# A fourth step of expert tables, after sample 13, and an output join in two parts

## The chip, the cores and the metric
One core of one Trainium2 chip. Engines: PE (TensorE), DVE (VectorE), ACT (ScalarE), POOL (GpSimd), and SP (SyncE), which issues the plain DMAs; POOL issues the indirect ones. The metric is device time in microseconds (us), lower is better.

## The reference
Sixteen samples of 128 tokens, width 256, pass through two decoder layers. Layer 0: a decayed linear recurrence, cross attention with 16 heads, a feed-forward in FP4. Layer 1: linear attention with a GELU feed-forward, cross attention, and a mixture of experts; a layer norm follows each. Only the last one matters here:

```
logits = xf @ gate_w + gate_b;  probs = softmax(logits)
gates, expert_idx = top_k(probs, 2)              # 2 of 8 experts for each of 2048 tokens
out = sum over the two experts of gate * (relu(x @ w1[e] + b1[e]) @ w2[e] + b2[e])
x = layernorm(x + out)
```

## The kernel before, in words
**Samples.** Six slots hold samples at a time; slot s runs samples s, s+6, s+12. Samples 13 to 16 are therefore the last to run. (Samples are numbered from 1 in the text and from 0 in the code, as n.)

**Routing.** When a sample is done, the router (`pe_router`, `dve_router`) finds its two experts for each token and the row that each pair takes in the expert's region of `xs_d` in HBM. POOL sends the sample's 128 rows there twice, by indirect DMA (L1744 in `pool_router`, then L1756 in `pool_second`, which waits for the first to land). The rank matmuls (L988, L989) give the positions and the running count of pairs per expert, `base`.

**Tiles.** The pairs are worked off in tiles of 128 rows of one expert. As the split over experts is known only at run time, a table (`dve_table`) lists row and expert for each tile. There is a table after each of STEPS = [8, 12, 16] samples, with 9, 8 and 22 tiles (39). The tables after 8 and 12 samples list full tiles alone, as many as there must be in any case; the last table lists all that is left. For a tile SP loads the rows (`rows`, L1885) and the expert's weights in two halves of 512 KB (`load up` L1890, `load down` L1894); PE transposes the rows (`turn`), multiplies by w1 (`up`) and by w2 (`down`); ACT applies bias, relu and the gate (L1615, L1608); POOL sends the 128 results back to the tokens' rows of `ys_d` by indirect DMA (`store`, L1778). Tiles of the first two tables share two buffers of weights, those of the last table have six (HOME, ROOM), four of which (in `PT` and `KB`) come free with the samples and are loaded at once ("early").

**Join.** `join_turns` orders the end. `fetch`: SP waits for the stores of all tiles and loads three rows for each token of a sample, the two expert results and the token with its expert biases, 384 KB (L1864). `add`: POOL adds the first result (L1766). `join`: DVE adds the second and takes mean and variance (L1362 to L1367), POOL the inverse root (L1626), and ACT subtracts the mean (L1589). `finish`: ACT scales (L1593) and SP writes the sample out (L1867). The 16 fetches stand first; then add n+1, join n, finish n-1 follow each other.

**Order.** Each engine runs its instructions in one fixed order. `orders_of` makes it: every piece of work has a listed cost and needs (`plan_*`), and at each step the piece that can start first in this plan is taken, the tiles' pieces last where two tie. The plan knows neither the data nor real times; on the chip an instruction waits for its semaphores, and all that stands behind it on that engine waits with it.

Of the kernel before, what the change touches and what calls it, by code (L numbers as in the profile page):

```python
# [7 lines left out]
ALU = mybir.AluOpType  # L8
# [38 lines left out]

STEPS = [8, 12, B]
SURE = [0, *(2 * m - E + 1 for m in STEPS[:-1]), 2 * B + E - 1]
# [3 lines left out]
REGION = B * P  # L53
NTMAX = max(TILES)
ZROWS = 2048

# [10 lines left out]
CONST = [("cos", DH), ("sin", DH), ("ident", P), ("block", P), ("mask8", HC), ("dest", 2 * B), ("dump", 8), ("iota", E), ("kkeep", 1),  # L67
         ("kminus", 1), ("before", P), ("region", E), ("tiles", NTMAX)]

# [421 lines left out]
def decoder_kernel(nc, xg, xTg, cTg, wts, w4gu, w4dn, rows, cols, const, moe_w, moe_b2, zeros, out):  # L491
# [14 lines left out]
    with ExitStack() as ctx:  # L506
# [47 lines left out]
        for buffers, width in ((XS, XW), (XST, D), (YB, D), (HM, EHC * P)):  # L554
            for i in range(2):
# [18 lines left out]
        base = sb("base", E)  # L574
        cnt = sb("cnt", 6, E + 1)
        below = sb("below", NTMAX, E)
        tcol = sb("tcol", 3, NTMAX)
# [25 lines left out]

        lg_ready, pr_ready, picked, idx_ready, tab_ready, directed, redirected, placed, halved, joined, var6, centred, root6, out_ready = (
            sem(n) for n in ("lg_ready", "pr_ready", "picked", "idx_ready", "tab_ready", "directed", "redirected", "placed",
                             "halved", "joined", "var6", "centred", "root6", "out_ready"))
        gated = sem("gated")
# [79 lines left out]
        def join_rows(n):  # L687
            if n < B // 2:
                return KB_all[:, 3 * D * n:3 * D * (n + 1)]
            j = n - B // 2  # L690
            return slot_rows[:, :, :, :].rearrange("p s a b -> p (s a b)")[:, 3 * D * j:3 * D * (j + 1)]

# [565 lines left out]
        def dve_router(k):  # L1258
            e = k.e
            for n in range(B):  # L1260
# [26 lines left out]
                k.wait_ge(filled[u.at], u.full)  # L1287
                run = base[:, :] if n else k_("region")
                placed = k.step(e.tensor_tensor(lg[:, :], ps[:, u.at, 0:E], run, ALU.add))
# [7 lines left out]
                for t in step_at(n):  # L1297
                    dve_table(k, t)
                    yield

        def dve_table(k, t):


            e, nt, full = k.e, TILES[t], t < len(STEPS) - 1
            c, end, begin, step, had, row0 = (cnt[:, i, 0:E] for i in range(6))
            region, top = k_("region"), float(E * REGION // P)
            hit, tiles = below[0:1, 0:nt, :], k_("tiles")[0:1, 0:nt]
# [4 lines left out]
            k.after(k.step(e.tensor_tensor(c, base[:, :], region, ALU.subtract)))  # L1312
            k.after(k.step(e.tensor_scalar(c, c, 1.0 / P, -half if full else half, ALU.mult, ALU.add)))
            k.after(k.step(e.tensor_scalar(c, c, ROUND, None, ALU.add)))
            k.after(k.step(e.tensor_scalar(c, c, ROUND, None, ALU.subtract)))
            if t:
                k.after(k.step(e.tensor_tensor(c, c, had, ALU.subtract)))
            k.after(k.step(e.tensor_tensor_scan(end, ones[:, 0:E], c, 0.0, ALU.mult, ALU.add)))
            k.step(e.tensor_tensor(hit, bc(end[0:1, :].unsqueeze(1), nt, E), bc(tiles.unsqueeze(2), nt, E), ALU.is_le))
            k.step(e.tensor_scalar(cnt[:, 5, E:E + 1], end[:, E - 1:E], -1.0, top, ALU.mult, ALU.add))  # L1320
            k.after(k.step(e.tensor_tensor(begin, end, c, ALU.subtract)))
            k.after(k.step(e.scalar_tensor_tensor(out=row0, in0=region, scalar=1.0 / P, in1=begin, op0=ALU.mult,
                                                  op1=ALU.subtract)))
            if t:
                k.after(k.step(e.tensor_tensor(row0, row0, had, ALU.add)))
            k.after(k.step(e.tensor_tensor(step, cnt[:, 5, 1:E + 1], row0, ALU.subtract)))
            k.after(k.step(e.tensor_reduce(owner, hit, AX.X, ALU.add)))
            k.after(k.step(e.tensor_tensor(hit, hit, bc(step[0:1, :].unsqueeze(1), nt, E), ALU.mult)))
            k.after(k.step(e.tensor_reduce(gone, hit, AX.X, ALU.add)))
            k.after(k.step(e.scalar_tensor_tensor(out=rows_, in0=gone, scalar=row0[0:1, 0:1], in1=tiles, op0=ALU.add,  # L1330
                                                  op1=ALU.add)))
            k.after(k.step(e.tensor_scalar(tab[t][0:1, 0, :], rows_, float(P), None, ALU.mult)))
            e.tensor_scalar(tab[t][0:1, 1, :], owner, float(E - 1), float(P), ALU.min, ALU.mult).then_inc(tab_ready, 1)
            if full:
                k.after(k.step(e.tensor_scalar(end, end, float(nt), None, ALU.min)))
                k.after(k.step(e.scalar_tensor_tensor(out=begin, in0=begin, scalar=float(nt), in1=end, op0=ALU.min,
                                                      op1=ALU.subtract)))
                if t:
                    k.after(k.step(e.tensor_tensor(had, had, begin, ALU.subtract)))
                else:  # L1340
                    k.after(k.step(e.tensor_scalar(had, begin, -1.0, None, ALU.mult)))

        def dve_bias(k):
# [9 lines left out]
        def dve_join(k):  # L1353
            e = k.e
            for what, n in join_turns():
                if what == "join":
                    v, rows_ = mv2[:, n % 8, :], join_rows(n)
                    x6 = rows_[:, 2 * D:3 * D]
                    k.wait_ge(halved, n + 1)
# [223 lines left out]

        def act_join(k):
            for what, n in join_turns():
                v, x6 = mv2[:, n % 8, :], join_rows(n)[:, 2 * D:3 * D]
                if what == "join":
                    k.wait_ge(var6, 2 * n + 2)
                    k.e.activation(x6, x6, ACT.Identity, scale=1.0, bias=v[:, 6:7]).then_inc(centred, 1)  # L1589
                elif what == "finish":  # L1590
                    k.wait_ge(centred, n + 1)
                    k.wait_ge(root6, n + 1)
                    k.e.activation(x6, x6, ACT.Identity, scale=v[:, 7:8], bias=0.0).then_inc(out_ready, 1)  # L1593
                yield

        def act_tiles(k):
# [163 lines left out]
        def pool_join(k):  # L1760
            for what, n in join_turns():
# [5 lines left out]
                elif what == "join":  # L1767
                    k.wait_ge(var6, 2 * n + 2)
                    pool_root(k, mv2[:, n % 8, :]).then_inc(root6, 1)
# [165 lines left out]
        def idle():  # L1935
            yield from ()
# [15 lines left out]
        @block.scalar  # L1952
        def _(e):
            k = Program(e, None)
            act_start(k)
            in_order("A", [*slots_of(k, act_sample), act_weights(k), act_fold(k), act_router(k), idle(), act_bias(k), act_join(k), idle(), act_tiles(k)])

# [87 lines left out]
```

## Time and profile before

| | us |
|---|---|
| median of 3 runs (995.23 to 997.38) | 996.99 |
| the profiled execution, its own time | 998.28 |
| its span, first to last instruction | 995.2 |
| PE busy in the span | 868.6 (87%) |
| DVE busy | 615.4 (62%) |
| ACT busy | 497.9 (50%) |
| POOL busy | 297.1 (30%) |

Times in the rows are microseconds from the start of the span. The engines' shares are means over stages which differ much: samples with the tiles of the first two tables up to 853.5, then the tiles of the last table, then the join. What a part costs is read in its own stage.

### The profile page before, as it was taken

The page shows a single profiled execution, that of the slowest core. Times are in us where ns is not written, and L with a number is a line of the kernel's source. Part 1 is how long each engine was busy: PE and PEld are TensorE (multiplying, and loading weights), DVE is VectorE, ACT ScalarE, POOL GpSimd, SP SyncE. Part 2 cuts the span into 40 slices and gives each one's busy share as a digit, 9 for nine tenths or more (in the row PEclk, how much of TensorE's full clock was granted, in tenths as well). Part 3 has the DMA queues.
Part 4 walks back from the last instruction along what each step waited for, and adds up shares of the span by engine and source line. Part 5 has one row for each costly group of instructions (what it writes and reads, how often), then busy time and mean ns, then how long its engine had stood idle before and what let it go on. Part 6 is the DMA issues. An engine that isn't in the chain of part 4 may idle for free.

```text
span 995.2 us, 19709 instructions
## 1 busy us (share of the span) xinstructions
PE 868.6 (87%) x7316; PEld 688.7 (69%) x7316; DVE 615.4 (62%) x1840; ACT 497.9 (50%) x1159; POOL 297.1 (30%) x478
## 2 busy tenths in 40 slices
PE   3669899999999899999999999999999999299950
PEld 2446668667777666777678777877877888289940
DVE  4998776676765768866848685778854434200016
ACT  2335446553656454553465545565555555045535
POOL 4423322222343123431213333232421214212236
PEclk9679999999999989999999999999999999689985
DMA  8996000000010000000000030231121226699836
GB/s 323 400 323 210 2 1 12 12 7 17 17 33 28 18 7 17 22 22 17 6 2 22 23 118 23 91 118 54 55 84 54 92 91 212 225 318 351 321 129 235
DMA packets 35950, 102.33 MB, mean 103 GB/s; under 512 B 4984, under 2 KB 20352, under 8 KB 35296
## 3 DMA queue, kind: packets, MB, share of 16 engines
q1 hardware_dynamic: 32448, 91.74, 27.0%
q0 software_dynamic: 3408, 9.34, 2.5%
q8 instruction: 58, 0.95, 0.4%
q14 instruction: 36, 0.29, 0.1%
HBM read 87.53 MB, written 33.35 MB: 121 GB/s over the span
## 4 chain that ended last, share of the span: by engine, by line
PE 63%; DVE 19%; ACT 7%; issue 6%; DMA 3%; POOL 1%; SPq 0%; ACTq 0%; DVEq 0%; POOLq 0%
PE ps L705 44%; PE ps L710 7%; PE ps L717 5%; PE ps L781 3%; DVE PT L1104 2%; DVE stat L1045 2%; ACT PT L1438 2%; ACT slot_rows L1438 1%; PE ps L848 1%; DMA xs_d<-X,idx 1%; PE ps L1006 1%; DVE sm L1061 1%; DVE PT L1069 1%; DMA KB<-xs_d 1%; DVE stat L1046 1%
## 5 line engine op out<-in xcount | busy, mean ns | idle before, releaser
L1626 POOL TENSOR_TENSOR stat<-stat,mhalf 128x1 f32<-128x1 f32 x112 | 67.1, 599 | 291.2 <-DVE stat L1047 291.1
L705 PE MATMUL ps<-wall,slot_rows 128*128 128x256 f32 (+1 forms) x448 | 132.3, 424 | 11.3 <-ACT KB L1465 8.9
L705 PEld LDWEIGHTS ps<-wall,slot_rows 128*128 128x128 f32 x448 | 79.1, 193 | 36.0 <-issue 22.8
L710 PE MATMUL ps<-cst,PT 128*128 128x128 f32 x512 | 73.4, 280 | 14.9 <-DVE PT L1104 4.2
L717 PE MATMUL ps<-KB 32*128 32x128 f32 (+1 forms) x2048 | 76.9, 287 | 7.2 <-DVE PT L1104 2.4
L1104 DVE TENSOR_REDUCE PT<-ps 128x8 f32<-128x1024 f32 x64 | 75.3, 1219 | 12.5 <-PE ps L717 12.4
L705 PE MATMUL ps<-wgu,slot_rows 128*128 128x352 f32 x256 | 82.1, 473 | 0.8 <-ACT slot_rows L1400 0.6
L717 PEld LDWEIGHTS ps<-KB 32*128 32x128 f32 (+1 forms) x2048 | 64.9, 190 | 25.7 <-issue 20.6
L705 PEld LDWEIGHTS ps<-slot_rows,wall 128*128 128x128 f32 x640 | 75.8, 193 | 8.5 <-issue 4.1
L705 PE MATMUL ps<-slot_rows,wall 128*128 128x128 f32 x640 | 79.6, 279 | 1.8 <-DVE KB L1165 0.9
L710 PEld LDWEIGHTS ps<-cst,PT 128*128 128x128 f32 x512 | 58.7, 143 | 30.6 <-issue 16.2
L705 PEld LDWEIGHTS ps<-wgu,slot_rows 128*128 128x128 f32 x256 | 48.9, 195 | 27.6 <-issue 4.8
L705 PE MATMUL ps<-wall,cT 128*128 128x512 f32 x128 | 64.0, 624 | 0.1
L1400 ACT COPY slot_rows<-ps 128x256 f32<-128x256 f32 x96 | 35.5, 378 | 49.3 <-PE ps L710 48.8
L705 PE MATMUL ps<-wall,PT 128*128 128x256 f32 x256 | 58.3, 381 | 1.2 <-ACT PT L1520 1.2
L1692 POOL TENSOR_TENSOR KB<-PT,sm 128x352 f32<-128x352 f32 x32 | 26.4, 826 | 95.3 <-DVE PT L1069 95.2
L705 PEld LDWEIGHTS ps<-wall,PT 128*128 128x128 f32 x256 | 47.4, 190 | 7.8 <-ACT PT L1520 1.4
L1045 DVE BATCH_NORM_STATS2 stat<-slot_rows 128x6 f32<-128x256 f32 x112 | 47.9, 427 | 3.8
L705 PE MATMUL ps<-wdn,PT 128*128 128x256 f32 x192 | 48.1, 392 | 0.3 <-ACT PT L1493 0.3
L705 PE MATMUL ps<-work,EW 128*128 128x128 f32 x368 | 45.2, 276 | 2.0 <-ACT PT L1438 1.7
L705 PEld LDWEIGHTS ps<-work,EW 128*128 128x128 f32 x368 | 43.0, 192 | 2.6 <-ACT PT L1438 1.9
L705 PE MATMUL ps<-EW,work 128*128 128x256 f32 x184 | 44.0, 382 | 0.6 <-DMA EW<-moe_w 0.6
(237 smaller groups left out, 1817.5 us busy)
## 6 DMA issues: line engine op xcount, KB each, us to landing
EW<-moe_w SPq DMA_DIRECT2D x23, 514.0 KB, 4.3
EW<-moe_w SPq DMA_DIRECT2D x23, 512.0 KB, 5.0
PT<-moe_w SPq DMA_DIRECT2D x12, 514.0 KB, 5.9
PT<-moe_w SPq DMA_DIRECT2D x12, 512.0 KB, 6.9
wall<-wts SPq DMA_DIRECT2D x1, 4104.0 KB, 20.4
work<-xs_d SPq DMA_DIRECT2D x25, 129.0 KB, 3.3
KB<-ys_d SPq DMA_DIRECT2D x8, 384.0 KB, 5.9
slot_rows<-ys_d SPq DMA_DIRECT2D x8, 384.0 KB, 9.3
```

Of the source, the lines that this page charges most:

```text
L705: last = k.e.matmul(o, a, b, start=(i == 0), stop=(i == len(pairs) - 1))
L710: last = k.e.transpose(ps[:, u.at, c * P:(c + 1) * P], src[:, c * P:(c + 1) * P], ident)
L717: last = k.e.matmul(ps[:, at, c * P:(c + 1) * P], lhsT[lane, c * P:(c + 1) * P], rhs[lane, c * P:(c + 1) * P], start=True, stop=True)
L781: last = k.e.matmul(ps[lane:lane + HR, u.at, c:c + P], VS[:, s, h * (DH + 1):h * (DH + 1) + HR], exps(s, a, i // HC)[:, i % HC * P:(i % HC ...
L848: last = k.e.transpose(ps[0:kw[i], u.at + i // 4, (i % 4) * P:(i % 4 + 1) * P], KB[s][:, i * P:i * P + kw[i]], ident)
L1006: k.e.matmul(ps[:, u.at, 0:D], gT[0:E, :], b2m[0:E, :], start=True, stop=True).then_inc(filled[u.at], 1)
L1045: k.after(k.step(e.bn_stats(v[:, 0:6], src)))
L1104: e.tensor_reduce(peak[:, 2 * p:2 * p + 2, :, DH], s4, AX.X, ALU.max).then_inc(emptied[u.at], 1)
L1400: k.e.copy(dst, v3(ps[:, u.at, 0:D], P)).then_inc(emptied[u.at], 1)
L1438: e.activation(v3(exps(s, a, p), 512), ps[:, u.at:u.at + 2, :], ACT.Exp, scale=DH ** -0.5).then_inc(emptied[u.at], 1)
L1626: return k.e.tensor_tensor(v[:, 7:8], v[:, 8:9], mhalf[:, :], ALU.pow)
L1692: e.tensor_tensor(h, y, bc(sm[:, s, j, 1, 0:m].unsqueeze(2), m, DH), ALU.mult).then_inc(gpsimd[s], 1)
```

## The change
- STEPS gets 13: the tables come after 8, 12, 13 and 16 samples and list 9, 8, 2 and 20 tiles, 39 as before.
- The last table lists tiles in two groups, first those that hold a pair of samples 1 to 13 (at most SHOWN = 33 tiles in all are then done), then the others. It works on 16 columns instead of 8, and its scratch lies in `w("oT")`.
- Fetches of samples 1 to 13 wait for the first 33 tiles only. The join runs as two parts, samples 1 to 13 and 14 to 16, so its pieces can stand between those of the last 6 tiles.
- The fetches of 14 to 16 stand in SP's order behind the output of sample 11 (n = 10).
- ACT has no part in the join any more: the last step is one DVE instruction, (x - mean) * root, and the instruction that negated the mean is gone. `centred` is gone too.
- Rows of the join lie elsewhere: ten samples in `slot_rows`, the rest from the end of `KB`.

```diff
-STEPS = [8, 12, B]
+STEPS = [8, 12, 13, B]
...
+SEEN = STEPS[-2]
+SHOWN = 2 * SEEN + E - 1
...
 def join_turns():
-    yield from (("fetch", n) for n in range(B))
-    yield "add", 0
-    for n in range(B):
-        if n < B - 1:
-            yield "add", n + 1
-        yield "join", n
-        if n:
-            yield "finish", n - 1
-    yield "finish", B - 1
+    for lo, hi in ((0, SEEN), (SEEN, B)):
+        if not lo:
+            yield from (("fetch", n) for n in range(lo, hi))
+        yield "add", lo
+        for n in range(lo, hi):
+            if n < hi - 1:
+                yield "add", n + 1
+            yield "join", n
+            if n == SEEN - 1:
+                yield from (("fetch", m) for m in range(SEEN, B))
+            if n > lo:
+                yield "finish", n - 1
+        yield "finish", hi - 1
+
+def tiles_of(n):
+    return SHOWN if n < SEEN else NT
...
 def plan_join():
-                        needs=[(n, "saved"), ("table", len(STEPS) - 1), *(("stored", x) for x in range(NT))])
+                        needs=[(n, "saved"), ("table", len(STEPS) - 1), *(("stored", x) for x in range(tiles_of(n)))])
-            yield piece(work=[("D", 1.4, None), ("a", 0.4, None), ("P", 0.57, (n, "last root"))], needs=[(n, "halved")],
-                        alone=True)
+            yield piece(work=[("D", 1.2, None), ("P", 0.57, (n, "last root"))], needs=[(n, "halved")], alone=True)
-            yield piece(work=[("A", 0.4, None), ("S", 0.5, None), ("Q", 0.4, None), ("L", 2.0, (n, "out"))],
+            yield piece(work=[("D", 0.42, None), ("S", 0.5, None), ("Q", 0.4, None), ("L", 2.0, (n, "out"))],
...
+        def dve_counts(k, out, half):
+            e = k.e
+            k.after(k.step(e.tensor_tensor(out, base[:, :], k_("region")[:, 0:E], ALU.subtract)))
+            k.after(k.step(e.tensor_scalar(out, out, 1.0 / P, half, ALU.mult, ALU.add)))
+            k.after(k.step(e.tensor_scalar(out, out, ROUND, None, ALU.add)))
+            k.after(k.step(e.tensor_scalar(out, out, ROUND, None, ALU.subtract)))
...
         def dve_table(k, t):
+            parts = 1 if full else 2
+            wide = parts * E
...
+                k.step(e.tensor_tensor(c[:, E:wide], c[:, E:wide], seen, ALU.subtract))
+                k.after(k.step(e.tensor_tensor(c[:, 0:E], seen, had, ALU.subtract)))
...
+            if not full:
+                k.after(k.step(e.tensor_scalar(gone, owner, float(E), -float(E), ALU.is_ge, ALU.mult)))
+                k.after(k.step(e.tensor_tensor(owner, owner, gone, ALU.add)))
...
+            if STEPS[t] == SEEN:
+                dve_counts(k, seen, half)
...
         def dve_join(k):
-                    e.tensor_scalar(v[:, 6:7], v[:, 6:7], -1.0, None, ALU.mult).then_inc(var6, 1)
+                elif what == "finish":
+                    k.wait_ge(root6, n + 1)
+                    e.tensor_scalar(x6, x6, v[:, 6:7], v[:, 7:8], ALU.subtract, ALU.mult).then_inc(out_ready, 1)
...
-        def act_join(k):
...
         def sp_join(k):
-                    for x in range(NT):
+                    for x in range(tiles_of(n)):
                         k.wait_ge(ys_stored[HOME["store"][x][0]], 16 * HOME["store"][x][2])
```

## Rows read from the trace of the kernel before

**Rows 1.** Busy time by stage: window and length, then PE PEld DVE ACT POOL, clock, DMA, GB/s.
```profile
787.00:800.00 13.00, 13.00 (x143) 11.80 (x143) 1.33 (x7) 8.90 (x21) 3.21 (x6) 1.00 0.51 161
843.00:853.50 10.50, 9.48 (x58) 8.01 (x56) 3.13 (x19) 4.32 (x14) 3.93 (x4) 1.00 0.59 194
853.50:873.00 19.50, 0.59 (x2) 0.18 (x2) 4.12 (x21) 0.06 (x1) 3.42 (x6) 0.54 0.72 263
873.00:876.00 3.00, 2.92 (x12) 2.50 (x13) 0.73 (x5) 0.93 (x4) 0.00 (x0) 0.50 1.01 311
888.00:950.00 62.00, 62.00 (x431) 57.69 (x430) 2.23 (x14) 33.20 (x119) 15.54 (x17) 1.00 0.87 312
```

**Rows 2.** The chain that ended last: start, us, what.
```profile
858.38 6.14 DMA xs_d<-X,idx
...
865.32 7.60 DMA KB<-xs_d
...
934.49 0.22 PE ps L710 x2
934.71 3.52 PE ps L705 x24
...
962.16 3.11 DMA KB<-ys_d
```

**Rows 3.** Time line 842 to 859: start, us, engine, line, what, idle before.
```profile
842.95 2.85 SPq L1894 DMA_DIRECT2D EW<-moe_w  x2
844.53 0.96 POOL L1778 DMA_INDIRECT ys_d<-work,place  x1 [0.31 <-issue]
850.55 1.97 PE L705 MATMUL ps<-EW,work 128*128 128x256 f32 x8 [0.58 <-DMA EW<-moe_w]
852.35 0.28 PE L988 MATMUL ps<-mask,cst 128*128 128x8 f32 x2
853.59 0.16 DVE L1312 TENSOR_TENSOR cnt<-base,cst 128x8 f32<-128x8 f32 x1
853.78 0.96 POOL L1778 DMA_INDIRECT ys_d<-work,place  x1 [1.59 <-ACT work L1608]
855.95 0.32 DVE L1327 TENSOR_REDUCE tcol<-below 1x22 f32<-1x176 f32 x1
857.50 0.17 DVE L1333 TENSOR_SCALAR tab<-tcol 1x22 uint32<-1x22 f32 x1
858.39 0.34 SPq L1890 DMA_DIRECT2D PT<-moe_w  x1
```

**Rows 4.** POOL's time line, two stores of tiles of the second table.
```profile
815.07 1.04 POOL L1778 DMA_INDIRECT ys_d<-work,place  x1 [1.91 <-ACT work L1608]
823.39 0.96 POOL L1778 DMA_INDIRECT ys_d<-work,place  x1 [7.28 <-ACT work L1608]
```

**Rows 5.** Time line of the last tiles (the first two lines: tiles 33 and 39).
```profile
938.26 0.47 ACT L1608 ACTIVATE KB<-ps,gate 128x256 f32<-128x256 f32 x1 [0.59 <-PE ps L705]
938.40 0.33 SPq L1894 DMA_DIRECT2D KB<-moe_w  x1
939.50 0.96 POOL L1778 DMA_INDIRECT ys_d<-KB,place  x1 [2.78 <-DVE place L1378]
...
959.67 0.96 POOL L1778 DMA_INDIRECT ys_d<-KB,place  x1 [0.77 <-ACT KB L1608]
962.16 3.65 SPq L1864 DMA_DIRECT2D KB<-ys_d  x8
```

**Rows 6.** DMA issues from 937 to 941 and after 960: count, KB each, median us to landing.
```profile
ys_d<-KB,place POOLq DMA_INDIRECT x1, 5.1
...
slot_rows<-ys_d SPq DMA_DIRECT2D x8, 384.0 KB, 9.3
```

**Rows 7.** The join's groups (by form): count, busy us, mean ns, idle before.
```profile
L1626 POOL TENSOR_TENSOR mv<-mv,mhalf 128x1 f32<-128x1 f32 x16 | 9.6, 603 | 2.9 <-DVE mv L1367 2.9
...
L1766 POOL TENSOR_TENSOR slot_rows<-slot_rows 128x256 f32<-128x256 f32 x8 | 5.8, 720 | 0.0
```

**Rows 8.** Time line of the join, its first and its last.
```profile
966.09 0.42 DVE L1362 TENSOR_TENSOR KB<-KB 128x256 f32<-128x256 f32 x1 [27.23 <-POOL KB L1766]
...
967.23 0.15 DVE L1366 TENSOR_SCALAR mv<-mv 128x1 f32<-128x1 f32 x1
967.30 0.14 DVE L1367 TENSOR_SCALAR mv<-mv 128x1 f32<-128x1 f32 x1
...
988.22 0.15 DVE L1366 TENSOR_SCALAR mv<-mv 128x1 f32<-128x1 f32 x1
```

**Rows 9.** One line's instructions: duration min/median/max in ns, first and last start.
```profile
L1056 DVE TENSOR_SCALAR X<-slot_rows,stat x16: 399/408/734, 244.7 to 842.3; 128x256 f32<-128x256 f32 x16
```

More of the change, by code:

```diff
@@ L67 @@
 CONST = [("cos", DH), ("sin", DH), ("ident", P), ("block", P), ("mask8", HC), ("dest", 2 * B), ("dump", 8), ("iota", E), ("kkeep", 1),
-         ("kminus", 1), ("before", P), ("region", E), ("tiles", NTMAX)]
+         ("kminus", 1), ("before", P), ("region", 2 * E), ("tiles", NTMAX)]
 def spans(table):
@@ L574, in decoder_kernel @@
         base = sb("base", E)
-        cnt = sb("cnt", 6, E + 1)
-        below = sb("below", NTMAX, E)
+        cnt = sb("cnt", 6, 2 * E + 1)
+        below = sb("below", max(TILES[:-1]), E)
         tcol = sb("tcol", 3, NTMAX)
@@ L1287, in dve_router @@
                 k.wait_ge(filled[u.at], u.full)
-                run = base[:, :] if n else k_("region")
+                run = base[:, :] if n else k_("region")[:, 0:E]
                 placed = k.step(e.tensor_tensor(lg[:, :], ps[:, u.at, 0:E], run, ALU.add))
@@ L1299, in dve_router @@
                     yield
+        def dve_counts(k, out, half):
[4 more added lines that the diff above has]
+            k.after(k.step(e.tensor_scalar(out, out, ROUND, None, ALU.subtract)))
         def dve_table(k, t):
             e, nt, full = k.e, TILES[t], t < len(STEPS) - 1
-            c, end, begin, step, had, row0 = (cnt[:, i, 0:E] for i in range(6))
-            region, top = k_("region"), float(E * REGION // P)
-            hit, tiles = below[0:1, 0:nt, :], k_("tiles")[0:1, 0:nt]
+            parts = 1 if full else 2
+            wide = parts * E
+            c, end, begin, step, gone0, row0 = (cnt[:, i, 0:wide] for i in range(6))
+            had, seen = cnt[:, 4, 0:E], cnt[:, 4, E:2 * E]
+            region, top = k_("region")[:, 0:wide], float(E * REGION // P)
+            late = v3(w("oT")[:, 0:nt * wide], wide)
+            hit, tiles = (below[0:1, 0:nt, :] if full else late[0:1, :, :]), k_("tiles")[0:1, 0:nt]
             owner, gone, rows_ = (tcol[0:1, i, 0:nt] for i in range(3))
@@ L1311, in dve_table @@
             k.wait_ge(emptied[u.at], u.out)
[L1312 to L1320, printed above, removed]
+            dve_counts(k, c[:, wide - E:wide], -half if full else half)
+            if full:
+                if t:
+                    k.after(k.step(e.tensor_tensor(c, c, had, ALU.subtract)))
+            else:
+                k.step(e.tensor_tensor(c[:, E:wide], c[:, E:wide], seen, ALU.subtract))
+                k.after(k.step(e.tensor_tensor(c[:, 0:E], seen, had, ALU.subtract)))
+            k.after(k.step(e.tensor_tensor_scan(end, ones[:, 0:wide], c, 0.0, ALU.mult, ALU.add)))
+            k.step(e.tensor_tensor(hit, bc(end[0:1, :].unsqueeze(1), nt, wide), bc(tiles.unsqueeze(2), nt, wide), ALU.is_le))
+            k.step(e.tensor_scalar(cnt[:, 5, wide:wide + 1], end[:, wide - 1:wide], -1.0, top, ALU.mult, ALU.add))
             k.after(k.step(e.tensor_tensor(begin, end, c, ALU.subtract)))
@@ L1324, in dve_table @@
             if t:
-                k.after(k.step(e.tensor_tensor(row0, row0, had, ALU.add)))
-            k.after(k.step(e.tensor_tensor(step, cnt[:, 5, 1:E + 1], row0, ALU.subtract)))
+                k.after(k.step(e.tensor_tensor(row0, row0, gone0, ALU.add)))
+            k.after(k.step(e.tensor_tensor(step, cnt[:, 5, 1:wide + 1], row0, ALU.subtract)))
             k.after(k.step(e.tensor_reduce(owner, hit, AX.X, ALU.add)))
-            k.after(k.step(e.tensor_tensor(hit, hit, bc(step[0:1, :].unsqueeze(1), nt, E), ALU.mult)))
+            k.after(k.step(e.tensor_tensor(hit, hit, bc(step[0:1, :].unsqueeze(1), nt, wide), ALU.mult)))
             k.after(k.step(e.tensor_reduce(gone, hit, AX.X, ALU.add)))
@@ L1582, in act_bias @@
                 yield
-        def act_join(k):
[L1585 to L1594, printed above, removed]
         def act_tiles(k):
@@ L1955, in _ @@
             act_start(k)
[L1956 removed]
+            in_order("A", [*slots_of(k, act_sample), act_weights(k), act_fold(k), act_router(k), idle(), act_bias(k), idle(), idle(), act_tiles(k)])
         @block.gpsimd
@@ L2022 @@
              "before": np.triu(np.ones((P, P), np.float32), 1),
-             "region": np.tile(np.arange(E, dtype=np.float32) * REGION, (P, 1)),
+             "region": np.tile(np.arange(E, dtype=np.float32) * REGION, (P, 2)),
              "dest": np.stack([8 * P + 3 * (P * n + np.arange(P)) + i for n in range(B)
```

20 lines of the change are left out of this document (11 added, 9 removed).

## The prediction

> **What bounds the kernel now.** I read the busy time by stage first. Up to 853.5 us PE is busy nearly without a break (13.0 of 13.0 us, later 9.5 of 10.5) at the full clock, and DVE has room (1.3 and 3.1 us). Then PE stands still for 19.5 us (0.59 busy). From 873 on it is busy without a break again (62.0 of 62.0), and the join has no PE work [rows 1]. The chain of waits says what each stretch hangs on: the second scatter of the last sample (6.1 us), the load of the first tile's rows (7.6), then PE alone, 0.22 + 3.52 = 3.74 us a tile, then the last store, a fetch (3.1) and 16 joins [rows 2]. The join's time line: the first variance stands at 967.23 + 0.15 = 967.38, the last at 988.37; that is 15 rounds of 1.40 us, and the span ends 6.83 us after the last one [rows 8].
>
> So the kernel ends with three stages in a row: PE idle, PE bound, then DVE and POOL bound with PE idle. The change touches all three.
>
> **Part 1: two tiles moved from the last step to the step after sample 13.** The PE-bound stage loses 2 x 3.74 = 7.5 us [rows 2]. The two tiles must run somewhere. Before 853.5 they would lengthen a full PE; in the idle 19.5 us they are free, needing 7.5 at most. Which it is, follows from the buffers. The second and first table's tiles share two pairs of weights. The last two down loads of before are issued from 842.95, and PE still waits 0.58 us for one at 850.55, the last product of the old 17 tiles, right before the rank matmul of sample 16 at 852.35 [rows 3]. Tile 19's down load can be issued only when that product has read its buffer (852.5); so its product falls about 858, into the idle stretch. Tile 18's up product can stand before the rank, and its store can stand on POOL in front of the second scatter. I charge 1.0 us for both together. Bounds: 0 (all in the gap) and, if PE's order has both tiles ahead of the rank, the tile pitch of that stage, 8.3 us each [rows 4], 16.6.
>
> The table of the last step is what the early weight loads wait for (last write 857.50, first load 858.39), and the first row load is behind 4 MB of those. It works on 20 x 16 = 320 elements in place of 22 x 8 = 176: four instructions of 0.32 at 176 and 0.16 at 8 (the first subtraction) [rows 3], so about 0.14 more each, 0.55; two more for the owner and one for the counts at 0.17 to 0.2, 0.5. Sum 1.05, on the path: 1.0. Bounds 0 (the row load waits for the scatter, not for the weights) to 1.5.
>
> The table after sample 13 and its four counts are about 22 small DVE instructions of some 0.2 us, 4.7 us, and stand beside full PE work with DVE busy 10 to 30% [rows 1]: nothing, at most 4.7 if every sample waited for them. The clock after the gap stays as it was (0.50 at 873, [rows 1]), since PE still stands idle for over 10 us; had it stayed at its upper level I would gain about 2.
>
> Sum of part 1: -7.5 + 1.0 + 1.0 = **-5.5**.
>
> **Part 2: the join of samples 1 to 13 beside the last six tiles.** All times here are on the clock of before, the shift of part 1 comes on top. Tile 33's result is in ACT at 938.26, its store issued at 939.50 [rows 5] and landed 5.1 us later [rows 6], 944.6. The last weight load is issued at 938.40 [rows 5], that is before: no load stands behind the fetches on SP. The first fetch then lands after about 3.2 (962.16 to POOL's add at 965.34; the chain has 3.1 [rows 2]), so 947.9. The later ones come about 1.1 us apart: the last eight, issued from 965.9 to 969.8, have a median of 9.3 [rows 6]; (967.8 + 9.3 - 965.3) / 11 = 1.07. That is faster than the rounds.
>
> The round: POOL does an add, 0.72, and a root, 0.60 [rows 7], 1.35 with the gaps. DVE goes from 966.09 to 967.30 = 1.20 without the negation that is removed [rows 8], plus the new last step, 0.41 (the nearest instruction, same form [rows 9]) and 0.05 for the semaphore: 1.66. Alone DVE would set 1.66 a round, against 1.40 before: the edit frees ACT, which was no bound, and loads DVE, which now is. In the 13 rounds four stores of tiles 36 to 39 come in on POOL, 0.96 + 0.31 = 1.27 each [rows 3]: POOL has 13 x 1.35 + 4 x 1.27 = 22.6, 1.74 a round. I take 1.74; below it 1.66, above it 2.0 (a store that stands before its result is there holds POOL 0.77 more, [rows 5]).
>
> First variance 947.9 + 2.0 (965.34 to 967.38) = 949.9. Thirteenth: + 12 x 1.74 = 970.8. The last store lands at 962.1, but SP's order puts fetch 14 behind the output of sample 11, whose last step ends at 969.1 + 0.4 = 969.5; with that output's own issue the fetch goes out at 970.1 and lands at 973.3. Variance 14 at 975.3, variance 16 at + 2 x 1.66 = 978.6. To the end 6.83 - 0.49 (ACT's last step) + 0.41 (DVE's) = 6.75: 985.4, against 995.2. Sum of part 2: **-9.8**. Of the 13 joins taken from behind the tiles, 13 x 1.40 = 18.2 us, about half comes back: rounds are longer, they don't fit beside six tiles (22.4 us), and the fetch of the last three waits in SP's order.
>
> The rest (larger constants, other addresses of the rows, the `oT` scratch) is a few hundred bytes a partition and free.
>
> **A rule against the change.** L1056, the form of the new step, lasts 408 ns [rows 9], as long as the two-source add of 0.42 [rows 8]: no sign in these rows that it runs in a faster mode. The Trainium skill, "SBUF — State Buffer", section "Who interferes with whom", says that a `tensor_scalar` on VectorE can enter a mode with both port pairs and then keeps GpSimd out for its whole length. The trace speaks against it, as far as equal durations show that. What it would cost is the third rival.
>
> **Sum.** -5.5 - 9.8 = -15.3. The profiled execution took 998.28 (span 995.2): 983.0. It lies 1.3 above the median of the runs, so as a median **981.7**.
>
> **Rivals.**
> 1. The last three alone are left (chance 0.15). Joins 1 to 13 end before the last store, and fetch 14 goes out at 962.16: variance 16 at 967.38 + 2 x 1.66 = 970.7, end 977.5, -17.8; with part 1 at -6.5, -24.2: 972.8. Against it: 13 rounds would need to fit between 949.9 and about 962, 1.0 each, less than DVE's own 1.20 [rows 8], unless the fetches of before came earlier. A mild form (rounds of 1.66) gives 979.
> 2. The two tiles run ahead of sample 16 (0.13). Then all of the 7.5 us is back in front, part 1 is 0, and the time 996.99 - 9.8 = 987.2. For it: the tiles' pieces filled PE in this stage before [rows 3].
> 3. DVE's last step and POOL's adds exclude each other (0.10). POOL's round is 1.35 + 0.41 = 1.76; 13 of them and four stores 28.0, 2.15 a round. Thirteenth variance 975.7, output 11 at 974.0, fetch 14 landed 977.8, variance 16 at 979.8 + 2 x 1.76 = 983.3, end 990.1, -5.1; with part 1 986.4. This is what the rule cited above would make.
> 4. The change doesn't do what it says (0.04): in the engines' order the first joins stand behind the last tile's pieces. Then 16 rounds of 1.66 from 967.38: variance 16 at 992.3, end 999.0, +3.8; with part 1 -1.7: 995.3, no change.
> 5. Slower (0.06): the scatter of sample 16 late. Mechanism: PE's order has tiles 18 and 19 whole before the rank matmul of sample 16, each waiting for weights in one of two buffers, 2 x 8.3 [rows 4]; POOL's order has both stores (0.77 + 0.96 each, [rows 5]) before the scatters, 3.5; the table 1.0. Together 21.1, so +13.6 after the two tiles, less 9.8: +3.8, 1000.8. It decides from where the first scatter comes over 17 us later than 855. For it only the 0.58 us wait; against it the buffers, which put tile 19's weights behind the rank, and the need for all of it at once.
>
> My own line, with its spread, has 0.52.
>
> **How the numbers follow.** About 0.2% (2 us) is what a measurement of this kernel can tell from no change. Faster: 0.52 + 0.15 + 0.13 + 0.10 = 0.90, and a little of rival 4: 0.91. Same 0.03, slower 0.06. The range goes from rival 1, 973, to just above rivals 2 and 3, 990; this holds part 2 at rounds of 2.0 (13th variance 973.9, so 3.1 later: 984.8) and part 1 at -2 as well.
>
> **What would show it.** Right: PE busy for two tiles between 853.5 and 873, the first row load's landing at 873 to 876 and 20 tiles after it; ACT without work after the last tile; the first add about 14 us before the last tile's result (953); rounds of 1.65 to 1.8 on DVE; fetch 14 issued after the output of sample 11 and well after the last store has landed; about 7 us from the last variance to the end. Wrong: a gap from sample 16's rank to the first tile longer than 22 us; POOL adds drawn out beside DVE's last steps; PE waiting among the last six tiles, which would mean that fetches take the DMA engines from weights; adds that begin only behind the last store.

## The result and the profile after

The changed kernel takes 982.70 us (median of 4 runs, 981.53 to 984.84), the kernel before beside it 996.11 (4 runs): ratio 0.9865, 95% interval 0.9843 to 0.9888. On a second chip session, with 5 runs against 15 of before, the ratio was 0.984 (0.9821 to 0.986). Forecast were 981.7, with 973 to 990 around it.

The page of the changed kernel, its head:

```profile
span 983.0 us, 19689 instructions
PE 868.5 (88%) x7316; PEld 688.0 (70%) x7316; DVE 629.5 (64%) x1868; ACT 483.5 (49%) x1127; POOL 298.2 (30%) x478
```

PE does the same work as before, ACT 14 us less, DVE 14 us more. Line numbers have moved: L705 is now L719, L710 L724, L1364 L1397, L1362 L1395, L1626 L1649, L1766 L1789, L1778 L1801, L1864 L1887, L1867 L1890, L1608 L1631; L1402 is DVE's new last step.

Busy time by stage, the same columns as in [rows 1] (853 to 873 is the stretch in which PE had 0.67 us of work before, at a mean clock of 0.55):

```profile
853.00:873.00 20.00, 9.51 (x57) 7.81 (x55) 4.74 (x20) 3.71 (x11) 5.82 (x9) 0.82 0.91 329
863.50:875.00 11.50, 0.26 (x2) 0.02 (x1) 0.52 (x2) 0.24 (x2) 0.96 (x1) 0.60 1.03 389
875.00:879.00 4.00, 3.95 (x17) 3.46 (x18) 0.70 (x5) 0.89 (x4) 0.00 (x0) 0.50 0.95 331
938.00:962.00 24.00, 14.17 (x91) 12.73 (x89) 15.63 (x45) 7.43 (x25) 16.79 (x23) 0.84 0.77 279
962.00:983.00 21.00, 0.00 (x0) 0.00 (x0) 11.02 (x38) 0.00 (x0) 9.41 (x15) 0.50 0.37 119
```

The two tiles run in the first line, beside a product of tile 17, then PE is idle until 875. The fourth line is what the change is about: DVE and POOL, 2.23 and 15.54 us busy in 62 beside the tiles before [rows 1], work on joins there. In the last 21 us DVE is busy for half the time; in a stretch of 21 us of the join before (967 to 988) DVE was busy for 17.99 and POOL for 18.61.

The chain of waits of the changed kernel over the idle stretch and at the seam between the two parts of the join (start, us, what), which answers to [rows 2]:

```profile
859.18 7.17 DMA xs_d<-X,idx
...
867.24 7.64 DMA KB<-xs_d
...
875.01 1.09 PE ps L724 x4
...
959.12 1.14 issue
960.25 0.97 DVE slot_rows L1395
961.22 0.02 issue
961.25 0.44 DVE mv L1397
...
967.00 0.33 SPq L1890
...
967.57 0.33 SPq L1887
967.90 0.05 issue
967.95 4.60 DMA KB<-ys_d
972.55 0.07 issue
972.62 0.73 POOL KB L1789
```

Time line of the changed kernel: tile 33's step on ACT, the first fetches, the first add (they answer to [rows 5, 8]):

```profile
932.03 0.47 ACT L1631 ACTIVATE work<-ps,gate 128x256 f32<-128x256 f32 x1 [0.59 <-PE ps L719]
933.26 0.96 POOL L1801 DMA_INDIRECT ys_d<-work,place  x1 [2.77 <-ACT work L1631]
939.06 5.68 SPq L1887 DMA_DIRECT2D slot_rows<-ys_d  x10
942.17 0.73 POOL L1789 TENSOR_TENSOR slot_rows<-slot_rows 128x256 f32<-128x256 f32 x1 [0.47 <-DMA slot_rows<-ys_d]
944.07 0.15 DVE L1399 TENSOR_SCALAR mv<-mv 128x1 f32<-128x1 f32 x1
```

The term that was to be watched is the round, from one variance (the end of L1399) to the next. Read from the time lines, the 12 rounds of samples 1 to 13 are 1.43, 3.63, 1.57, 3.31, 1.52, 1.52, 1.53, 3.35, 1.52, 1.52, 1.52, 1.52: 23.94 us, 2.00 in the mean. A second profile of the same kernel has 22.5. Four stores fall among these rounds, in two pairs: the first of a pair at the start of a plain round (1.57, 1.52), the second late in the long round behind it (3.31, 3.35). The first store of the second pair, between two variances 1.52 apart:

```profile
957.05 0.15 DVE L1399 TENSOR_SCALAR mv<-mv 128x1 f32<-128x1 f32 x1
957.27 1.16 POOL L1801 DMA_INDIRECT ys_d<-work,place  x1 [0.17 <-issue]
```

and the long round, with the second store in it:

```profile
958.47 0.58 POOL L1649 TENSOR_TENSOR mv<-mv,mhalf 128x1 f32<-128x1 f32 x1
958.58 0.15 DVE L1399 TENSOR_SCALAR mv<-mv 128x1 f32<-128x1 f32 x1
959.02 0.71 POOL L1789 TENSOR_TENSOR slot_rows<-slot_rows 128x256 f32<-128x256 f32 x1
959.08 1.25 DVE L1402 TENSOR_SCALAR slot_rows<-slot_rows,mv 128x256 f32<-128x256 f32 x1 [0.35 <-POOL mv L1649]
959.70 0.66 POOL L1649 TENSOR_TENSOR mv<-mv,mhalf 128x1 f32<-128x1 f32 x1
960.22 0.71 POOL L1789 TENSOR_TENSOR slot_rows<-slot_rows 128x256 f32<-128x256 f32 x1
960.25 0.96 DVE L1395 TENSOR_TENSOR slot_rows<-slot_rows 128x256 f32<-128x256 f32 x1
961.11 1.04 POOL L1801 DMA_INDIRECT ys_d<-work,place  x1 [0.18 <-issue]
961.25 0.43 DVE L1397 BATCH_NORM_STATS2 mv<-slot_rows 128x6 f32<-128x256 f32 x1
```

The root at 958.47 is late because a store stood in front of it. DVE's last step begins 0.06 after a POOL add and takes 1.25 instead of 0.40; it ends with POOL's root. The next add on DVE begins 0.04 after a POOL add and takes 0.96 instead of 0.42. The last store, whose result ACT had ready at 952.7, is issued at 961.11.

### The profile page after: what moved, and what is told of

The parts are those of the page before. It is cut to its first block, busy times and chain, and to the rows that moved or that the text cites. A ratio compares the mean times of both kernels' runs of the same rounds, so it can differ in the third digit from the quotient of the medians.

```text
span 983.0 us, 19689 instructions
## 1 busy us (share of the span) xinstructions
PE 868.5 (88%) x7316; PEld 688.0 (70%) x7316; DVE 629.5 (64%) x1868; ACT 483.5 (49%) x1127; POOL 298.2 (30%) x478
## 4 chain that ended last, share of the span: by engine, by line
PE 59%; DVE 19%; ACT 7%; issue 6%; DMA 5%; POOL 2%; SPq 1%; POOLq 0%; ACTq 0%; DVEq 0%
PE ps L719 41%; PE ps L724 7%; PE ps L731 5%; PE ps L795 3%; DMA xs_d<-X,idx 2%; DVE PT L1118 2%; DVE stat L1059 2%; ACT PT L1473 2%; ACT slot_rows L1473 1%; PE ps L862 1%; DVE sm L1075 1%; DVE PT L1083 1%; PE ps L1020 1%; DMA KB<-xs_d 1%; DMA slot_rows<-ys_d 1%
## 5 line engine op out<-in xcount | busy, mean ns | idle before, releaser
L1649 POOL TENSOR_TENSOR stat<-stat,mhalf 128x1 f32<-128x1 f32 x112 | 67.1, 600 | 292.9 <-DVE stat L1061 292.8
L719 PE MATMUL ps<-wall,slot_rows 128*128 128x256 f32 (+1 forms) x448 | 132.1, 423 | 11.6 <-ACT KB L1500 9.1
L719 PEld LDWEIGHTS ps<-wall,slot_rows 128*128 128x128 f32 x448 | 79.0, 192 | 36.2 <-issue 23.0
L724 PE MATMUL ps<-cst,PT 128*128 128x128 f32 x512 | 73.5, 280 | 15.3 <-DVE PT L1118 4.2
L719 PE MATMUL ps<-wgu,slot_rows 128*128 128x352 f32 x256 | 82.1, 473 | 0.8 <-ACT slot_rows L1435 0.6
L719 PEld LDWEIGHTS ps<-slot_rows,wall 128*128 128x128 f32 x640 | 75.8, 193 | 8.5 <-issue 4.0
L719 PE MATMUL ps<-slot_rows,wall 128*128 128x128 f32 x640 | 79.6, 279 | 1.8 <-DVE KB L1179 0.9
L724 PEld LDWEIGHTS ps<-cst,PT 128*128 128x128 f32 x512 | 58.8, 143 | 31.0 <-issue 16.2
L719 PEld LDWEIGHTS ps<-wgu,slot_rows 128*128 128x128 f32 x256 | 48.9, 195 | 27.5 <-issue 4.6
L719 PE MATMUL ps<-wall,cT 128*128 128x512 f32 x128 | 64.3, 627 | 0.1
L719 PE MATMUL ps<-wall,PT 128*128 128x256 f32 x256 | 58.3, 381 | 1.2 <-ACT PT L1555 1.2
L719 PEld LDWEIGHTS ps<-wall,PT 128*128 128x128 f32 x256 | 47.4, 190 | 7.8 <-ACT PT L1555 1.4
L719 PE MATMUL ps<-work,EW 128*128 128x128 f32 x400 | 49.3, 276 | 2.9 <-ACT PT L1473 1.7
L719 PEld LDWEIGHTS ps<-work,EW 128*128 128x128 f32 x400 | 46.7, 192 | 3.8 <-ACT PT L1473 1.9
L719 PE MATMUL ps<-EW,work 128*128 128x256 f32 x200 | 47.9, 382 | 1.2 <-DMA EW<-moe_w 1.2
L719 PE MATMUL ps<-wdn,PT 128*128 128x256 f32 x192 | 48.1, 393 | 0.3 <-ACT PT L1528 0.3
```

The costliest lines, as they stand in the source:

```text
L719: last = k.e.matmul(o, a, b, start=(i == 0), stop=(i == len(pairs) - 1))
L724: last = k.e.transpose(ps[:, u.at, c * P:(c + 1) * P], src[:, c * P:(c + 1) * P], ident)
L1649: return k.e.tensor_tensor(v[:, 7:8], v[:, 8:9], mhalf[:, :], ALU.pow)
```

## The experiments

All ratios are to the kernel before, run beside each; they are not exactly the quotients of the medians. Milestones that no single line shows are read from the time lines of each profiled execution, us:

| kernel | row indices of sample 16 to first tile's PE | tile 31 on ACT to last variance | 12 rounds | time, ratio (95% interval) |
|---|---|---|---|---|
| before | 19.5 | 57.6 | 16.9 | |
| changed | 22.8 | 51.6 | 23.9 | 0.9865 (0.9843 to 0.9888) |
| changed, again | 23.0 | 49.5 | 22.5 | 0.984 (0.9821 to 0.986) |
| third step alone | 22.0 | 58.3 | 17.5 | 0.9932 (0.9908 to 0.9955) |
| no third step | 21.0 | 48.4 | (11) 21.4 | 0.9933 (0.991 to 0.9956) |
| last step on ACT | 21.7 | 50.3 | 21.4 | 0.9897 (0.9874 to 0.9919) |
| fetches early | 22.6 | 47.3 | 21.7 | 0.9854 (0.9832 to 0.9876) |
| serial join, last step on DVE | 19.4 | 59.2 | 18.0 | 1.0005 (0.9989 to 1.002) |
| fetches early, one pipeline | 23.1 | 47.3 | 23.2 | 0.9816 (0.979 to 0.9841) |
| the same, last step on ACT | 23.2 | 45.2 | 21.7 | 0.9812 (0.9788 to 0.9836) |
| the same, again | 22.9 | 45.9 | 22.3 | 0.9826 (0.9803 to 0.9849) |
| changed, scatter first | 21.6 | 51.1 | 23.0 | 0.9868 (0.9848 to 0.9889) |
| all together | 23.0 | 45.2 | 21.9 | 0.9815 (0.9798 to 0.9832) |

**The third step alone.**

```diff
 # the kernel before
-STEPS = [8, 12, B]
+STEPS = [8, 12, 13, B]
```

> The kernel before with one edit, STEPS = [8, 12, 13, B]; join, ACT's part and the 8-column table as before. My theory (two tiles move into PE's idle stretch, the rest of part 1 is 1 us of order and 1 to 1.5 us of the wider table): -7.5 + 1.0 = -6.5, about 989.5 beside 996. Rival (the tiles run ahead of sample 16 and only shift the idle stretch): within 1.5 us of before, 995 or more. Rival (the gain of the change is all in the join): 996.

Measured 988.43 against 993.96: the medians differ by 5.5 us, and the ratio, 0.9932, makes it 6.8 (4.5 to 9.1). Forecast were 6.5. Part 1 is real, of the size forecast, and both rivals fall. PE in the idle stretch of this kernel:

```profile
853.00:873.00 20.00, 8.22 (x45) 6.57 (x44) 2.18 (x10) 3.79 (x12) 4.74 (x7) 0.79 0.93 342
```

The stretch from the row indices to the first tile grows by 2.5 us all the same in this one profile, with the narrow table: the two tiles are not free.

**No third step.**

```diff
 # the changed kernel
-STEPS = [8, 12, 13, B]
+STEPS = [8, 12, B]
```

> The changed kernel with STEPS = [8, 12, B], so SEEN is 12 and SHOWN 31: 22 tiles in the last step, the last 8 beside the joins of 12 samples, four joins behind. My theory by the rows of the changed kernel (rounds of 2.0 us beside the tiles, 1.52 without stores, the fetch of the next behind the output of sample 10): first variance about 8 us ahead in relation to the last tile, twelfth about 965, the last about 974, so about 983, hardly slower than the change although the two tiles are not moved. Rival (the gains of the two parts add up, -6.5 for the step): 989.

Measured 986.87, ratio 0.9933: -6.7 us, against the 13 that I had worked out. (The profiled execution was the fastest of its five at 985.63.) A miss, and the trace shows two reasons. SP's time line, the first and the last fetches:

```profile
937.20 3.62 SPq L1887 DMA_DIRECT2D slot_rows<-ys_d  x4
...
967.13 1.75 SPq L1887 DMA_DIRECT2D KB<-ys_d  x4
```

The first fetches go out at 937.20, but the first add waits until 942.42 for them, 5.2 us in place of 3.1: with eight tiles left, weights are still on their way (the last two loads land at 938.97 and 940.25). And the last four fetches go out only at 967.13, when the last store has landed, which POOL issued at 964.44, 6.6 us after ACT's step had ended, since joins stood before it; the round at the seam is 6.39. So the two parts of the change add up: 0.9932 and 0.9933 alone, 0.9865 and 0.984 together, though this kernel is not quite part 2 alone (the joins of 12 samples beside 8 tiles, not of 13 beside 6). It also shows the wider table by itself. From the row indices to the table's last write it is 4.13 to 4.16 us in the three profiles with the narrow table and 5.3 to 5.65 in the ten with the wide one, here 5.47: 1.2 to 1.5 us.

**The last step on ACT again.**

```diff
 # the changed kernel; act_join as before, L1366 followed by the negation
-                elif what == "finish":
-                    k.wait_ge(root6, n + 1)
-                    e.tensor_scalar(x6, x6, v[:, 6:7], v[:, 7:8], ALU.subtract, ALU.mult).then_inc(out_ready, 1)
+                    e.tensor_scalar(v[:, 6:7], v[:, 6:7], -1.0, None, ALU.mult).then_inc(var6, 1)
```

> The changed kernel with the mean and the scale back on ACT (negation on DVE, two ACT instructions). Theory A (in the rounds of 2.0 us DVE's last step and POOL's adds hold each other up): rounds fall to POOL's 1.74, up to 3 us off the thirteenth variance. Theory B (ACT is the tighter engine beside the tiles: 2.2 us a tile plus 2.1 rounds of 1.0 us is 4.3 us in 3.74): the last tiles come 2 to 4 us late and the run is 984 to 987. Neither: 982.7.

Measured 984.18, ratio 0.9897. In the trace rounds without a store alternate between 1.26 and 1.55 (mean 1.41), where the change has 1.52. But each of the four stores now has a long round of its own (2.95, 2.58, 2.58, 2.58), where the change has two for four stores (3.31, 3.35). Over the 12 rounds a store costs (21.4 - 12 x 1.41) / 4 = 1.1 us here, and (21.7 - 12 x 1.52) / 4 = 0.9 with the step on DVE (21.7 in the profile of the next experiment, whose rows were all in time). So the 12 rounds are 0.3 us shorter: theory A promised up to 3 and is not confirmed. The last tiles come at 940.4, 945.9 and 949.8 on ACT, the first of these gaps 5.4 in place of 3.7. That is what theory B describes, but it isn't what the end waits for: the last store has landed at 957.7 and the last fetches go out at 963.58, in SP's order. The gap between variances 13 and 14 is 6.05 here, 1.5 more than in the change, and takes back what the rounds gave; why these fetches went out 0.3 us behind variance 13, and not 0.6 ahead of it, was not looked into. The time says that nothing is won. Its interval overlaps with the change's first one and not with the second (0.9821 to 0.986), across sessions.

**The fetches of the last three earlier.**

```diff
 # the changed kernel, join_turns
-            if n == SEEN - 1:
+            if n == SEEN - 6:
                 yield from (("fetch", m) for m in range(SEEN, B))
```

> The changed kernel with the fetches of samples 14 to 16 five outputs earlier in SP's order (behind the output of sample 6). My theory (the bubble from the 13th variance at 968.2 to the 14th at 972.7 comes from SP's order; the last store has landed about 956): the bubble of 3.1 us and part of the slow landings go, 979 to 980. Rival (DMA traffic sets when those rows land, or DVE and POOL set the end anyway): 982 to 983.

Measured 980.25, ratio 0.9854. In the trace the fetches go out at 960.93, when the last store has landed, and the gap between variances 13 and 14 is 3.29 in place of 4.58 and 4.42; the 12 rounds were 21.7, since no rows came late. The bubble shrinks by 1.2, not by 3.1. What is left of it is the restart of the pipeline: add 14 stands on POOL behind root 13. The intervals overlap with the change's, so the time alone does not show a gain; the gap in the trace does.

**The serial join with its last step on DVE.**

```diff
 # the kernel before: plan and act_join changed as in the change, join_turns not
+                elif what == "finish":
+                    k.wait_ge(root6, n + 1)
+                    e.tensor_scalar(x6, x6, v[:, 6:7], v[:, 7:8], ALU.subtract, ALU.mult).then_inc(out_ready, 1)
```

> The kernel before with one edit, the last step of the join on DVE and ACT out of it; all joins still behind the last tile, no store among them. The term of my sum: a round of 1.66 in place of 1.40, so +3.8. By the rounds without a store in the changed kernel's trace it is 1.52, so +1.8. Rival (POOL sets the round, DVE's extra work costs nothing): 0.

Measured ratio 1.0005 (0.9989 to 1.002). The last 13 of 15 rounds are 1.52 or 1.53, and first to last variance is 22.60 against 20.99: +1.6 in the trace, which the time can just not tell from nothing. DVE's add never takes longer than 0.425 here:

```profile
L1361 DVE TENSOR_TENSOR KB<-KB x8: 412/419/425, 964.3 to 974.7; 128x256 f32<-128x256 f32 x8
```

One last step begins 0.37 after a POOL add and takes 0.49; the others take 0.40 to 0.41. My 1.66 was too long because it counted a last step with its 0.41: the next instruction begins 0.31 after it.

**One pipeline, and the small step on DVE with ACT.** Both have the early fetches; the second also has the last step on ACT, in one instruction.

```diff
 # join_turns of both
+    for n in range(B):
+        if n == SEEN - 6:
+            yield from (("fetch", m) for m in range(SEEN, B))
+        if n < B - 1:
+            yield "add", n + 1
+        yield "join", n
+        if n:
+            yield "finish", n - 1
 # the second, dve_join and act_join at "finish"
+                    e.scalar_tensor_tensor(out=v[:, 8:9], in0=v[:, 6:7], scalar=-1.0, in1=v[:, 7:8], op0=ALU.mult,
+                                           op1=ALU.mult).then_inc(centred, 1)
+                    k.e.activation(x6, x6, ACT.Identity, scale=v[:, 7:8], bias=v[:, 8:9]).then_inc(out_ready, 1)
```

> The changed kernel itself, as the measure for the others of this chip: 14 us less than the kernel before (ratio 0.9865 so far).

> The changed kernel with the fetches early and one pipeline of joins, last step on DVE. Both bubbles at the seam (4.6 us in the changed kernel, 3.3 with the early fetches alone, against a round of 1.5) should go: 3 us below the changed kernel, 1.8 of it by the pipeline. Rival (the stores of the last tiles, late in POOL's order, hold the last fetches): the bubble moves and less than 1 us is won over the early fetches alone.

> The changed kernel with the fetches of 14 to 16 behind the output of sample 6, one pipeline of joins (add 14 stands before the root of 13), and the last step as one small DVE instruction and one ACT instruction. Rounds without a store at POOL's 1.41 in place of 1.52, and a store costs about 1.2 in place of up to 1.8, if DVE's 256-wide last step and POOL's adds hold each other: 1.5 to 3 us below the same kernel with the last step on DVE. Rival (ACT beside the tiles is the tighter engine): no gain over it.

The change had 981.20 (0.984), one pipeline 979.65 (0.9816), with ACT 977.79 (0.9812). The three intervals overlap; the traces show more. The seam is gone in both (1.52 and 1.27 between variances 13 and 14). Without ACT, part of that was lost at the start of the join, where the rows of samples 2 and 3 came late (rounds of 1.76 and 2.52), so that tile 31 to the last variance stayed at 47.3. With ACT it is 45.2, 2.1 less, but 1.5 of these are the same two rounds, which were 1.20 and 1.59 there, and 0.4 are the last three. The ten rounds from variance 3 to 13, with the four stores, take 18.9 us in both. They take 18.9 in all five profiles with the step on DVE and four stores among the rounds, and in all three that have it on ACT in one instruction (18.5 with two ACT instructions). So the gain of 1.5 to 3 us that I expected from ACT is not shown: beside the tiles the step's place makes no difference. What these ten rounds take is about POOL's own work, 10 x 1.35 + 4 x 1.27 = 18.6 by the figures of the prediction. DVE's 256-wide add is never held with the small step:

```profile
L1393 DVE TENSOR_TENSOR slot_rows<-slot_rows x10: 411/413/426, 941.9 to 958.2; 128x256 f32<-128x256 f32 x10
```

and in the changed kernel, with its own last step, both are:

```profile
L1395 DVE TENSOR_TENSOR slot_rows<-slot_rows x10: 414/423/959, 942.9 to 962.3; 128x256 f32<-128x256 f32 x10
```

(the add) and, for its last step,

```profile
L1402 DVE TENSOR_SCALAR slot_rows<-slot_rows,mv x10: 403/404/1410, 945.6 to 965.0; 128x256 f32<-128x256 f32 x10
```

**The scatter first, and all together.**

```diff
 # plan_tiles, "store"
-                        needs=[y, ("M", "placed", x)], alone=True)
+                        needs=[y, ("M", "placed", x), *[(B - 1, "sent")] * (x == SURE[-2] - 3)], alone=True)
```

> The changed kernel, with the store of tile 17 put behind the second scatter of sample 16 in POOL's order (an extra need in the plan). In the changed kernel's trace the idle stretch from sample 16's row indices (852.21) to the first tile's transpose (875.01) is 22.8 us, 3.3 more than before. Theory A (the store between the two scatters delays the second by 2.1 us and with it the row loads): the stretch shrinks to about 20.8 and the run is 2 us under the changed kernel, 0.982 of before. Rival B (the rows land when the 4 MB of early weights ahead of them have, and those wait for the wider table): the second scatter comes 2 us earlier, the stretch stays at 22 to 23, no gain.

> The same edit in the kernel with the fetches early, one pipeline of joins and the last step on ACT, the candidate for the best version: by theory A 2 us under that one, about 0.979 of before; by rival B the same as that one, 0.981.

> The kernel with the fetches early, one pipeline and the last step on ACT again, on this chip, beside the two others: 0.981 of before.

No gain: 0.9868 beside 0.9865 and 0.984, and 0.9815 beside 0.9812 and 0.9826. But the edit did not do what it was to do, so its time does not decide between the theories. (Its stretch of 21.6 is no sign of a gain: the kernel with the last step on ACT, in which nothing of this stage was changed, has 21.7.) The store went behind the second scatter, another one still stood before the first:

```profile
851.08 0.96 POOL L1802 DMA_INDIRECT ys_d<-work,place  x1 [5.24 <-ACT work L1632]
852.03 0.20 POOL L1766 COPY X<-cst 128x1 f32<-128x1 f32 x1
852.52 0.98 POOL L1768 DMA_INDIRECT xs_d<-X,idx  x1 [0.28 <-POOL X L1766]
855.65 0.18 POOL L1777 COPY X<-cst 128x1 f32<-128x1 f32 x1 [2.15 <-DMA xs_d<-X,idx]
856.23 0.98 POOL L1780 DMA_INDIRECT xs_d<-X,idx  x1 [0.28 <-POOL X L1778]
```

The first scatter is now 2.9 us behind the row indices (849.61), where it had been 1.7, and the second 6.6, where it had been 7.0 and 6.5.

The landings in the other profiles answer the question all the same. In the kernel without the third step the second scatter has landed at 859.06, and the first row load goes out only at 863.73, when SP has issued the early weights (the last weight load and the row load: start, then KB and us to landing):

```profile
862.49 0.33 SPq L1917 DMA_DIRECT2D KB<-moe_w  x1
863.73 2.54 SPq L1908 DMA_DIRECT2D KB<-xs_d  x3
KB<-moe_w SPq DMA_DIRECT2D x1, 512.0 KB, 8.9
KB<-xs_d SPq DMA_DIRECT2D x1, 129.0 KB, 8.0
```

With the early fetches the scatter lands at 866.74 and the row load goes out at 867.56, behind it:

```profile
863.71 0.51 SPq L1917 DMA_DIRECT2D KB<-moe_w  x1
867.56 0.34 SPq L1908 DMA_DIRECT2D KB<-xs_d  x1
KB<-moe_w SPq DMA_DIRECT2D x1, 512.0 KB, 10.4
KB<-xs_d SPq DMA_DIRECT2D x1, 129.0 KB, 6.9
```

The row load is issued 1.2 us behind the last weight load in the one and 3.9 in the other, and its rows land 0.35 and 0.34 us behind that load's. In all eight profiles that show both landings it is 0.34 to 0.44, for row loads issued 1.2 to 3.9 us behind. So the rows come when the 4 MB of weights have come, and an earlier scatter would have won nothing: rival B. The eight weight loads take 14.2 and 14.3 us from the first issue to the last landing in the two of these profiles without the third step, and 14.8 to 16.1 in the six with it. That, and the later table, is the growth of the stretch. What lengthens the loads (the two tiles' own weights, their stores, the scatter) no run separates.

The best version is the one with early fetches, one pipeline and the last step on ACT: 976.10 and 977.79 on two chip sessions, ratios 0.9826 and 0.9812, 17 to 19 us under the kernel before by the ratios (the times of before were 994.9 and 997.6) and 3.4 under the change in the same session, with intervals that overlap. The pair of this section parts clearly: with the scatter edit in both, the three edits together take 981.48 to 976.57, 0.9868 (0.9848 to 0.9889) to 0.9815 (0.9798 to 0.9832). Most of it is the seam.

## Why the prediction was right

The mechanism was that of the forecast in both parts, and the total too: 982.7 for 981.7. How near it came is partly luck: a gain and a loss that the sum lacked cancelled, and the profiled execution of the change, from which the steps below are read, is the slowest of its four runs, 2.1 us above their median, so that the miss in the profile is 3.1 us where the medians show 1.0. By its own steps, in the spans of the two profiled executions (995.2 and 983.0, -12.2, for -15.3; the rest of the 13.4 us between their own times, 998.28 and 984.84, lies outside the spans):

- **First tile of the last step at +2.0.** 875.01 against 873.05, as forecast, but made of other pieces. The way from sample 16's row indices to the first tile grew by 3.3 to 3.5 in the change's two profiles; the row indices themselves were earlier. They stand at 850.4 in the mean of the ten profiles with the third step (848.7 to 852.2) and at 852.1 in the three without it (850.9 to 853.5). The wider table has 1.2 to 1.5 of it (1.05 forecast). The rest, 1.8 to 2.0 here, is the longer way of the early weights with two more tiles in front; by the spread of the profiles, 21.6 to 23.2 in the ten with the third step, it is good to about 1 us. Tiles 18 and 19 stood where the buffers said: their w2 products began at 857.99 and 861.17. What I had not seen is that PE's order also puts tile 17's product, which before stood right in front of the rank matmul [rows 3], behind it (854.47, rank 851.05); only tile 18's transpose is new ahead of it. That product takes 2.0 us, which fits the 1.7 by which the row indices come earlier in the mean. Its store then comes between the two scatters. The bound that I gave at 0, that the row load waits for the scatter and not for the weights, is refuted by the landings above. So a gain and a loss of about 2 us each, both missing in my sum, cancelled.
- **Two tiles less.** From the first transpose to the last tile's step on ACT 77.2 us against 85.4: -8.2 for -7.5.
- **First variance.** 12.2 us after tile 33's step on ACT (11.7 in the second profile), for 11.6. The store landed after 5.8 and the fetch after 3.1.
- **The rounds, the step that was mis-sized.** 2.00 and 1.87 in place of 1.74: 23.9 and 22.5 us for 20.9. Most of the difference is one landing. I had the fetches come 1.1 us apart, faster than the rounds; in the first profile the rows of the third sample landed 3.6 us after the second's (POOL waited 2.36), and the first two rounds took 5.1 us where they take 2.8 with the rows in time: 2.3 lost there, 0.8 in the second profile. The kernel with the third step alone, whose fetches meet neither stores nor weights, has the same gap at 2.5, so the tiles beside are not its only cause; what is, stays open. With what the first two rounds lost taken off, the 12 rounds are 21.7 in all five profiles with the step on DVE and 13 joins beside six tiles.
- **The rest of that step, 21.7 for 20.9.** A plain round is shorter than I had it, 1.52 for 1.66, as the serial experiment shows without any store, and a store costs 0.9, where my 1.74 had room for four at 0.24 over DVE's 1.66. I had the right bound, POOL's work, but spread it over 13 rounds, and between the first and the 13th variance there are 12: 12 x 1.35 + 4 x 1.27 = 21.3. DVE's instructions are drawn out beside POOL's in the two long rounds, but the place of the last step doesn't change the ten rounds with the stores, 18.9 either way. So what my third rival described is there, and its price, 2.15 a round, is not.
- **The seam.** From variance 13 to 14 4.58 and 4.42 for 4.5; the last two rounds 3.44 for 3.3; the end 6.85 after the last variance for 6.75. That the last fetches wait in SP's order was right. But behind it lies a second cause that I had not seen, the last store: its result is ready at 952.7 and POOL issues it at 961.11, behind eight pieces of joins. With the early fetches it is what decides (fetches at 960.93), and without the third step it costs most.

The first, second, fourth and fifth rivals fall: the joins were not all hidden, the tiles didn't run ahead of sample 16, the first add came 10.0 us before the last tile's step on ACT, and the first scatter went out at 853.94, not 17 us later than before. Two of my signs of being wrong came true without the forecast failing: from sample 16's rank (851.05) to the first tile it is 24.0 us, more than the 22 that I had set as the limit (20.7 before), since the two tiles and the wider table lengthen that stretch; and instructions are drawn out where POOL's adds and DVE's last steps meet, above all those of DVE. (The 14 in my list of signs was a slip: its own working, 947.9 - 5.5 against 958.4 - 5.5, gives 10.5.) On the rule of the Trainium skill, "SBUF — State Buffer", section "Who interferes with whom": the rows that I set against it don't refute it. The step lasts 0.40 when no POOL add runs at its start, or one that is about to end, and 1.25 or 1.41 when it starts 0.06 to 0.08 behind the start of one. The rule makes the loser wait for the other's whole instruction, and the time lines agree only in part. With the early fetches a step that starts 0.06 behind an add which a second add follows takes 0.80 and ends 0.15 after the first; where a root follows, the step ends 0.60 and 0.75 after the add, the first of them beside the root's end (960.33 and 960.36). That ports are the reason no run here shows.

## What to carry to other kernels

When a serial tail moves beside a busy stage, price the queue that both share: here a store from the other stage costs the tail 0.9 to 1.2 us, up to its own time in POOL's queue, and the tail holds the last store back by 8.4. Divide a sum over rounds by the number of rounds that it covers. Put what the end waits for ahead of tail work in the in-order queues: with the last fetches that is shown here by the gap at the seam, with the last store it is an idea that no run tested. The duration of an instruction can depend on what the other engine has just begun; read the longest duration in a group, not the median alone. But an instruction that is drawn out costs nothing by that alone: move it away and see whether the rounds change, and compare the same rounds, since a late landing can look like the gain.

## What the runs showed of the hardware

- A 128x256 `tensor_scalar` on DVE takes 0.40 us, and up to 1.41 when it begins just behind a POOL add of two tiles in SBUF; a two-source DVE add 0.42 and up to 0.96. In the serial join, where no DVE instruction starts so close behind a POOL add, the longest are 0.49 and 0.425.
- Rows of 129 KB, loaded behind eight weight loads of 0.5 MB each, landed 0.34 to 0.44 us after the last of these in eight profiles, whether they were issued 1.2 or 3.9 us behind it.
- Two profiles of one kernel differ by up to 3.3 us at a point 850 us into the run, with the same program; single profiles can't settle a term of 2 us that begins there, differences inside one stage can.
